# One-hot stationary for 18 fetched node tiles, and the zero fill issued by ScalarE in the two-stack passes

## What is computed

```python
deg = segment_sum(ones, edge_dst, n)
norm = dinv[edge_src] * dinv[edge_dst]          # dinv = deg ** -0.5
root = einsum('nf,kfg->nkg', x, root_w)
for t in range(3):
    h = einsum('nf,kfg->nkg', x, init_w) if t == 0 else einsum('nkf,kfg->nkg', out, w)
    msg = h[edge_src] * norm[:, None, None]
    h = segment_sum(msg, edge_dst, n)           # the sum over edges
    out = relu(h + root + b)
```

## Time and profile before

| what | value |
|---|---|
| median of 3 timed runs | 3352.11 us (3344.53 to 3356.41) |
| the profiled execution | 3317.19 us, of which its span is 3315.3 |
| pass 0, first to last dense product | 1022.50 to 1471.34 us |
| pass 1 | 1471.34 to 1951.58 us |
| passes 2 to 4 | 1951.58 to some 2764 us |
| busy share of the span | PE 95%, DVE 40%, POOL 25%, ACT 23% |

### The profile page before, as it was taken

How to read it: one execution, slowest core, us unless ns; L and a number is a source line. 1 busy time by engine, 2 the same in 40 slices (tenths; PEclk the granted TensorE clock), 3 DMA queues, 4 the chain that set the end, 5 groups by cost and what they waited for, 6 DMA issues and landing times. The chain is left out here.

```text
span 3315.3 us, 51940 instructions
## 1 busy us (share of the span) xinstructions
PE 3133.6 (95%) x18657; PEld 1902.1 (57%) x18658; DVE 1341.3 (40%) x5159; ACT 771.9 (23%) x1620; POOL 834.1 (25%) x808
## 2 busy tenths in 40 slices
PE   7897999999999999998999999999999999929998
PEld 4464666665655666655666655555555556616775
DVE  7846778777762222222222212222221004624443
ACT  3444555555540000000000000000000002513333
POOL 3100000000003666626566610000000000654555
PEclk9896999999999999999999999999999999959999
DMA  7221554654738777766777768888889996436886
GB/s 192 80 66 60 185 212 161 239 216 161 247 162 314 243 242 242 255 218 213 239 231 249 236 221 282 290 291 292 291 291 321 303 302 195 148 129 176 203 199 138
DMA packets 244598, 723.87 MB, mean 218 GB/s; under 512 B 35343, under 2 KB 153347, under 8 KB 242354
## 3 DMA queue, kind: packets, MB, share of 16 engines
q1 hardware_dynamic: 181140, 609.25, 54.9%
q0 software_dynamic: 48256, 99.18, 10.8%
q10 hardware_dynamic: 15006, 12.82, 1.4%
HBM read 542.84 MB, written 189.35 MB: 221 GB/s over the span
## 5 line engine op out<-in xcount | busy, mean ns | idle before, releaser
L1831 PE MATMUL first_sum<-stage,split 128*128 128x448 f16 x4704 | 949.7, 354 | 1.9 <-DMA split<-fresh_d 1.9
L1831 PE MATMUL first_sum<-stage,other 128*128 128x448 f16 x3332 | 687.2, 353 | 0.0
L1831 PEld LDWEIGHTS first_sum<-stage,split 128*128 128x128 f16 x4704 | 450.1, 98 | 374.3 <-issue 5.3
L1781 PE MATMUL first_sum<-stage,other 128*128 128x448 f16 x2744 | 648.9, 354 | 0.2 <-ACT stage L1323 0.2
L1308 POOL DMA_INDIRECT stage<-fresh_d,lane_two x272 | 261.5, 961 | 1088.1 <-DMA fresh_d<-split 933.4
L1831 PEld LDWEIGHTS first_sum<-stage,other 128*128 128x128 f16 x3332 | 315.1, 98 | 244.7 <-issue 1.4
L1323 ACT ACTIVATE stage<-group_ps 128x392 f16<-128x392 f32 x784 | 385.6, 497 | 295.4 <-PE group_ps L1770 292.1
L1467 DVE TENSOR_SCALAR place<-iota_col,rel 128x196 f16<-128x196 f16 x1568 | 349.3, 266 | 0.0
L1781 PEld LDWEIGHTS first_sum<-stage,other 128*128 128x128 f16 x2744 | 253.7, 98 | 139.4 <-issue 2.0
L1308 POOL DMA_INDIRECT stage<-later_d,lane_two x272 | 261.6, 962 | 217.7 <-PE group_ps L1873 122.5
L1464 DVE TENSOR_TENSOR lanes<-iota_two,lane_two 128x256 f16<-128x256 f16 x784 | 225.7, 288 | 80.8 <-PE group_ps L1770 68.9
(11 more groups left out here) (383 smaller groups left out, 3019.6 us busy)
## 6 DMA issues: line engine op xcount, KB each, us to landing
stage<-adj_d SPq DMA_DIRECT2D x434, 784.0 KB, 4.2
adj_d<-stage SPq DMA_DIRECT2D x14, 5488.0 KB, 18.4
row_d<-slow_rows SPq DMA_DIRECT2D x12, 3340.5 KB, 29.9
other<-pack_d SPq DMA_DIRECT2D x38, 898.0 KB, 4.8
slot_rows<-row_d SPq DMA_DIRECT2D x38, 393.0 KB, 5.6
stage<-root_d SPq DMA_DIRECT2D x28, 448.0 KB, 7.0
xnT_d<-other SPq DMA_DIRECT2D x14, 448.0 KB, 4.2
split<-root_d SPq DMA_DIRECT2D x14, 448.0 KB, 3.9
```

What stands on the lines that cost most here:

```text
L1781: m = mm(acc[b][k][:, 0:WIN], other[:, h, half, k * P:(k + 1) * P], stage[b][:, h, :], start=(h == 0 and half == 0), stop=(h == TILES - 1 ...
L1831: m = mm(acc[b][k][:, 0:WIN], side(t)[:, h, part, k * P:(k + 1) * P], ring[:, i, r, :], start=(h == 0 and part == 0), stop=(h == TILES - 1 ...
```

## The change

The fetched nodes are cut in tiles of 128 instead of strips of 112, and there are 18 of them, 2304 nodes for 1792. Each has 19 chunks: 342 gathers a pass for 272. Windows 5 to 13 are dense, nine for ten; window 5 only in its last 384 columns, as the first 64 belong to the fetched tile 17. In a chunk the one-hot is now the stationary operand and the gathered rows, high and low parts side by side, are the 512 moving columns: one product for four. The sums then have nodes on partitions. ACT (`sums_high`) and DVE (`sums_low`) read them from the bank, scaled, PE turns them with two fp32 products, and DVE adds the roots. One bank holds the sums of all node tiles in turn, so between two node tiles three tiles without a chunk stand in `Course`.

The zero fill is no longer issued by SP in the build but by ACT, six parts in each two-stack pass, at tile 22 of the windows 1 to 6 of the pass. Roots of fetched nodes come per node tile. SP issues the stores of rows at other places, ahead of the ring piece of their step. The setting up of the list takes 3 gathers for 4 on POOL and 10 small transfers for 17 on SP.

```diff
-UNITS = 4
-STRIP = 112
-STRIPS = WIN // STRIP
-STRIP_GROUPS = STRIP // G
-CHUNK = 17
-LISTED = UNITS * STRIPS * CHUNK
+SPARSE = 18
+FIRST_DENSE = SPARSE * P // WIN
+OVERLAP = SPARSE * P - FIRST_DENSE * WIN
+CHUNK = 19
+ABREAST = P // SPARSE
+GATHERS = -(-CHUNK // ABREAST)
+LISTED = SPARSE * CHUNK
...
-    BEGIN, TAIL, LEAD, SETTLE, AFTER, APART = 28, 22, 10, 6, 8, 2
+    BEGIN, TAIL, LEAD, GAP = 30, 30, 10, 3
+    TURN, ADD, PROJECT, AFTER, APART = 3, 5, 9, 8, 2
 
     def __init__(self, windows):
         self.tiles = windows * TILES
-        self.chunk_at = [self.BEGIN + c * (self.tiles - self.BEGIN - self.TAIL) // LISTED for c in range(LISTED)]
-        self.strip_end = [self.chunk_at[(s + 1) * CHUNK - 1] + 2 for s in range(UNITS * STRIPS)]
-        self.row_at = {}
-        for pair in range(UNITS // 2):
-            for u in range(SUB):
-                self.row_at[(pair, u)] = self.strip_end[pair * 2 * STRIPS + -(-(u + 1) * P // STRIP) - 1] + self.SETTLE
+        span = self.tiles - self.BEGIN - self.TAIL
+        self.chunk_at = []
+        for s in range(SPARSE):
+            first, after = (self.BEGIN + n * span // SPARSE for n in (s, s + 1))
+            self.chunk_at += [first + c * (after - first - self.GAP) // (CHUNK - 1) for c in range(CHUNK)]
+        self.summed_at = [self.chunk_at[(s + 1) * CHUNK - 1] for s in range(SPARSE)]
+        self.row_at = {s: at + self.PROJECT for s, at in enumerate(self.summed_at)}
         for n in range(windows):
-            for place, u in enumerate(TAKEN[n % 2]):
-                self.row_at[((n + UNITS) // 2, u)] = (n + 1) * TILES + self.AFTER + self.APART * place
-        self.row_order = sorted(self.row_at, key=lambda row: (self.row_at[row], row))
+            w = n + FIRST_DENSE
+            for place, j in enumerate(fresh_tiles(w)):
+                self.row_at[j] = (n + 1) * TILES + self.AFTER + self.APART * place
...
     def piece_after(self, x):
-        return x // PT + PIECES + 1
+        return x // PT + PIECES - 1
...
-                    if w < CHUNKS:
-                        sp.wait_ge(c_z, 1)
-                        flat = row_d.rearrange("r c -> (r c)").rearrange("(p n f x) -> p n f x", p=P, f=FOLD, x=BLANK)
-                        sp.dma_start(flat[:, w, :, :], blank.unsqueeze(1).broadcast_to([P, FOLD, BLANK])).then_inc(c_blank, 16)
...
+                def sparse_roots(t, s):
+                    S = t * SPARSE + s
+                    if S >= 2:
+                        sp.wait_ge(s_v, S - 1)
+                    sp.dma_start(rin_s[:, s % 2, :, :], root1_d.rearrange("p (k n) -> p k n", k=2)[:, :, s * P:(s + 1) * P]).then_inc(s_in[s % 2], 16)
...
+                def stored_at(n):
+                    at = courses[0].piece_after(courses[0].row_at[SOME[n][-1]] + 2)
+                    return max(at, (ND - 1) * PIECES) if n < PARTED else at
...
                         M = t * ND * PIECES + m
+                        for some in range(len(SOME)):
+                            if M == stored_at(some):
+                                some_out(some)
                         if M >= PIECES:
                             sp.wait_ge(p_free, M - (PIECES - 1))
                             sp.dma_start(ring[:, i, :, :].rearrange("p t n -> p (t n)"), adj_d[DENSE[n], :, i * PT * WIN:(i + 1) * PT * WIN]).then_inc(p_in[i], 16)
...
                     for c in range(LISTED):
                         g = t * LISTED + c
                         if g >= RING:
                             pool.wait_ge(s_used, g - (RING - 1))
                             pool.wait_ge(s_row[g % RING], 16 * (g // RING))
+                        at = listed_at(*divmod(c, CHUNK))
                         nc.gpsimd.indirect_dma_start(got[:, g % RING, :, :].rearrange("p s c -> p (s c)"), None, tables_d[t].rearrange("p j s c -> (p j) (s c)"),
-                                                     bass.IndirectOffsetOnAxis(ap=tab_row[:, c:c + 1], axis=0)).then_inc(s_row[g % RING], 16)
+                                                     bass.IndirectOffsetOnAxis(ap=tab_row[:, at:at + 1], axis=0)).then_inc(s_row[g % RING], 16)
                 for r in range(RING):
...
+                def sums_high(t, s):
+                    S = t * SPARSE + s
+                    if S >= 2:
+                        act.wait_ge(s_pt, S - 1)
+                    act.wait_ge(s_used, t * LISTED + (s + 1) * CHUNK)
+                    nc.scalar.activation(rows_s[:, S % 2, :], group_ps[0][:, 0:D], ACT.Copy, scale=dinv[:, s:s + 1]).then_inc(s_hi, 1)
+
+                def cleared(w):
+                    flat = row_d.rearrange("r c -> (r c)").rearrange("(p n f x) -> p n f x", p=P, f=FOLD, x=BLANK)
+                    act.dma_start(flat[:, w, :, :], blank.unsqueeze(1).broadcast_to([P, FOLD, BLANK])).then_inc(c_blank, 16)
...
                     course = courses[t]
                     for x in range(course.tiles):
+                        if x % TILES == 22 and 1 <= x // TILES <= CHUNKS // 2:
+                            cleared(t * (CHUNKS // 2) + x // TILES - 1)
                         if t == 1:
-                            for n, pair, u in courses[0].rows(x + course.tiles):
-                                row_high(0, n, pair, u)
-                        for n, pair, u in course.rows(x):
-                            row_high(t, n, pair, u)
+                            for n, j in courses[0].rows(x + course.tiles):
+                                row_high(0, n, j)
+                        for s in course.summed(x):
+                            sums_high(t, s)
+                        for n, j in course.rows(x):
...
+                def sums_low(t, s):
+                    S = t * SPARSE + s
+                    one = rows_s[:, S % 2, :]
+                    dve.wait_ge(s_hi, S + 1)
+                    nc.vector.scalar_tensor_tensor(one, group_ps[0][:, D:2 * D], dinv[:, s:s + 1], one, ALU.mult, ALU.add).then_inc(s_ev, 1)
+
+                def sums_hidden(t, s):
+                    S = t * SPARSE + s
+                    one = hid_s[:, S % HELD, :, :]
+                    dve.wait_ge(s_in[S % 2], 16 * (S // 2 + 1))
+                    dve.wait_ge(s_pt, S + 1)
+                    nc.vector.tensor_tensor(one, group_ps[1][:, 0:D].rearrange("p (k n) -> p k n", k=2), rin_s[:, S % 2, :, :], ALU.add).then_inc(s_v, 1)
...
+                    mm(group_ps[0][:, :], hot[:, g % HOTS, :], got[:, g % RING, :, :].rearrange("p s c -> p (s c)"), start=(first == 0),
+                       stop=(first == CHUNK - 1), skip_group_check=True).then_inc(s_used, 1)
+
+                def sums_turned(t, s):
+                    S = t * SPARSE + s
+                    pe.wait_ge(s_ev, S + 1)
+                    if S >= 1:
+                        pe.wait_ge(s_v, S)
                     for k in range(2):
-                        for part in range(2):
-                            m = mm(group_ps[S % 2][:, k * D:k * D + STRIP], got[:, g % RING, part, k * P:(k + 1) * P], hot[:, g % HOTS, :],
-                                   start=(first == 0 and k == 0 and part == 0), stop=(first == CHUNK - 1 and part == 1), skip_group_check=True)
-                    m.then_inc(s_used, 1)
+                        m = nc.tensor.transpose(group_ps[1][:, k * P:(k + 1) * P], rows_s[:, S % 2, k * P:(k + 1) * P], ident[:, :])
+                    m.then_inc(s_pt, 1)
 
...
-                        m = tile_sums(t, n % 2, h, i, r)
+                        m = tile_sums(t, W % 2, h, i, r, OVERLAP if n == 0 else 0)
...
                         for c in course.chunks(x):
                             chunk(t, c)
+                        for s in course.summed(x - Course.TURN):
+                            sums_turned(t, s)
```

388 lines of the change are left out of this document (193 added, 195 removed).

## The result

The changed kernel took 3523.2 us (median of 4, 3521.2 to 3532.1), the kernel before beside it 3348.7 (4 runs, 3344.5 to 3356.4): a ratio of 1.052, interval 1.0495 to 1.0552. Forecast were 3376 us and a range that ended at 3410. The sign was right; 147 us were missing. The profiled run took 3532.1 us, span 3530.3.

The account below looks back on a forecast made before the run. GpSimd's gathers, 342 x 1.262 = 431.6 us a pass, were taken to become the bound. Pass 0 +23.6, pass 1 0, fills and the rest 0 made +24 on the median 3352.1: 3376 us, range 3358 to 3410.

Parts of the forecast that it names:

- 333 pitches later: 420.2: Pass 0: the last gather starts 333 pitches of 1.262 us, 420.2 us, after the ninth, at 1465.9.
- 0 and +20 us: Zero fills moved into the two-stack passes: worth between 0 and +20 us through longer gather landings; taken as 0.
- PE's sum and the bound: Two-stack passes: PE's sum falls 19 us a pass, but GpSimd's 342 gathers, 431.6 us, become the bound.
- the fills choke the gathers: Rival, two-stack passes: landings over 10.1 us make GpSimd stand still, 26 us a pass, 3428 us; chance 0.09.
- The issue costs what a transfer cost SyncE, 0.43 us: ScalarE's fill issues in the passes: 0.43 us each, before rows that come one in several us, so 0.
- nobody holds it: GpSimd's gathers in the catching-up stretch: starts 1.26 us apart with nobody holding it, so a pitch of 1.262 us.
- The 120.9: Pass 0 of the kernel before: GpSimd stands 120.9 us waiting for PE, the cover to watch.
- Between two node tiles PE has three tiles (2.3 us) in which ScalarE and VectorE must read the sum bank: no wait.: Node tile boundaries: ScalarE (0.47 us) and VectorE, much the same, read the bank within 2.3 us; PE waits 0.
- The session of the measurement some 8 either way.: Range of the whole kernel's time: the measurement session shifts it some 8 us either way.
- VectorE holds GpSimd off: Rival, gathers: a 256 ns one-hot before each makes the pitch 1.5, +80 us a pass, 3530 us; chance 0.01.
- What would show it.: Signs: gathers back to back, 0.30 between, releaser "issue"; PE waiting some 40 us for gathers in pass 0; pass 0 about 472 us.

Follow-up runs that it names:

- run 6: The kernel before, unedited, profiled beside the other runs on the same chip: 3317.1 us.
- run 8: The changed kernel with the zero fill issued by SyncE in the build again, timed beside the unedited changed kernel: 3339.3 us, ratio 1.007 to the kernel before.
- run 1: The changed kernel with the zero fill issued by SyncE in the build again, nothing else different: 3337.7 us, kernel before 3312.3.
- run 14: The changed kernel with the fill in the build, two sum banks, later turning and 12 buffers for fetched rows: 3330.2 us, ratio 1.0037 to the kernel before.
- run 13: The changed kernel with the fill in the build, a hand-made late bank release, two sum banks and turning 5 tiles later: 3540.8 us, ratio 1.051.
- run 5: The changed kernel, unedited, timed again beside the kernel before: 3384.2 us, ratio 1.020.
- run 2: The kernel before with only the zero fill moved to ScalarE, 12 pieces in the two-stack passes: 3322.1 us.

## Why the prediction was wrong

The changed kernel came 174 us above the kernel before, 24 were forecast. Of the rest 43 are what it loses in the quick groups too (3384.2 less 3317.1 is 67), the fills above all; 107 go with a condition that the forecast had not. Two steps failed that the time shows: that nobody holds GpSimd, so that its last gather comes "333 pitches later: 420.2", which took 491.2 us; and the fills at "0 and +20 us", which cost 45.

- *PE's sum and the bound.* Right. With the fill in the build and the increments on time the kernel takes 3339.3 for 3317.1, +22, where the sum said +24. Part of that closeness is luck: against the trace of before in the same group (run 6) the two passes are 30 us longer, for 24, and the rest of the kernel is 5 shorter. Pass 0 is 471.3 (forecast 472.4), pass 1 486.5 (480.3). In the first trace the product of 512 columns has its next neighbour 0.22 us after its start (1265.81 to 1266.03), as scaled. GpSimd, in runs 8 and 1:

```profile
L1325 POOL DMA_INDIRECT stage<-fresh_d,lane_two x342: 942/946/1160, 1020.8 to 1458.4; - x171
...
  issue: 134.0, 440
  PE group_ps L1913: 78.9, 206
...
L1325 POOL DMA_INDIRECT stage<-later_d,lane_two x342: 940/946/1362, 1507.1 to 1940.0; - x171
```

  In pass 1 of run 1 341 pitches in 432.9 us are 1.269, for 1.262. In pass 0 of run 8 the last gather starts 441.6 us into the pass, for 443.4. In pass 1 the first comes 17.7 us in, for 20.6, and the last 452.9, for 450.9; the pass is 6 us longer all the same, as the product of the last gather follows 8.1 us behind it (1941.0 to 1949.07) and not 3.9: PE is still at the chunks before it, and does not wait.
- *The bound tested by its size.* Fewer gathers, 304, gave 25 us against run 8, which only made up for what the change costs; spread by the time that PE has for them they gave 17 more, passes of 447.1 and 468.7 in place of 471.3 and 486.5.
- *The fills, "between 0 and +20 us; I take 0".* They cost 45 (3384.2 less 3339.3), well over the range's 20. The rival "the fills choke the gathers" had the mechanism, at 0.09 and 52 us; twelve buffers gave 33 back. With twelve buffers the fills still cost 21 (3351.1 less the 3330.2 of run 14, which has two banks and later turning besides), so some 24 of the 45 hung on the ring's depth. The evidence against it was its weak point: the fill's load is less than the ring's on average, but it comes beside the ring and not in its place, and gathers went from 4.0 to 7.7 us. "The issue costs what a transfer cost SyncE, 0.43 us" was a second error: the fill's own issue takes 0.4, and it is the next ones on its queue that take up to 6.4. The Trainium skill (DMA: Bandwidth & Descriptors, SWDGE vs HWDGE vs iDMA) says that a DMA engine goes round its queues in turn; that the fills would then cost 0 was drawn from it and is not on the page, and the measured 45 decide against it.
- *"nobody holds it", and so a pitch of 1.262 from the ninth gather to the last.* This is the step that failed in the first measurement, 71 of the 73 us in pass 0 and 80 of the 82 in pass 1. It needs PE's increment to be seen at once, each time that a gather waits for a buffer. The cover for it had gone: before, 271 pitches are 342 us of the 415 between the first gather and the last (1026.8 to 1442.0), so GpSimd had 73 us of slack in pass 0. The 120.9 that the prediction reads as its waiting for PE hold 160 waits, and in each the 0.30 that stand between any two gathers. In the changed kernel no slack is left, and the late releases, 131 us in both passes, go into the passes.
- *"Between two node tiles PE has three tiles (2.3 us) in which ScalarE and VectorE must read the sum bank: no wait."* This failed too, with 50.8 us of PE's waits, 6.20 at the place shown. It needs PE's increment to be seen at once and ScalarE to be free. With both, run 8 shows 0.2 us at 36 boundaries. But PE's time was not what set the passes, and without these waits, though with more of its increments late, run 13's passes are as long.
- *What the late increments cost outside the passes.* Against run 5 the span is 147 us longer: 106 in the passes, 34 behind the one-stack passes and 7 before pass 0. The 34 all lie in the first part of the final stage (the windows of the first measurement and of run 5):

```profile
2949.50:3190.00 240.50, 142.60 (x681) 104.54 (x679) 107.12 (x421) 76.36 (x158) 98.51 (x106) 0.79 0.41 135
```

```profile
2836.40:3043.00 206.60, 132.39 (x681) 98.41 (x679) 107.06 (x421) 76.09 (x158) 98.80 (x106) 0.83 0.48 158
```

  There GpSimd writes rows by indirect DMA, and ScalarE reads PE's sums (L2338, L2364) over 0.5 us late in 9 of 28 places, up to 4.7 us; in run 5 in none. The kernel before has this stage too, and its measurements differ by 32 us (3349 to 3317); that these are the same loss is not shown, as it was never traced in that condition. The 7 us are within what the other traces differ by (pass 0 starts at 1016 to 1024 us).
- *The clock of PE* is no term of the prediction. In the first measurement PE is busy 945.7 us in the two passes for 914.4 in run 5 and 897.2 in run 8, with the same products, at a granted clock of 0.95, 0.97 and 0.99. After the waits of 6.20 and 5.48 us shown above it stood at the lower of its two levels (0.61 us for a product of 0.38). Where GpSimd sets the pass, this falls into time that PE would have waited, so it has no price of its own here.
- *"The session of the measurement some 8 either way."* The kernel before alone spread from 3312 to 3371. That the profiled run stood 35 us under the median was a sign: I put the difference on the median, as if it added to both kernels alike.
- *VectorE holds GpSimd off*: no. Gathers beside more one-hots take 946 ns in the median (952 before).
- *What would show it.* The gathers "back to back with 0.30 between" are true of run 8: of all its gaps between gathers 2 in pass 0 and 8 in pass 1 are longer than 0.32 us, the longest in front of the first chunk. The releaser is not always "issue": the 78.9 us in 206 waits for PE in the rows above are, but for some 17, these same 0.30. PE's wait for gathers is 29.9 us in pass 0 (some 40 forecast).

## What to carry to other kernels

A stage is as robust as its tightest round trip: when an edit takes the slack from the second engine, and its buffers are released by another's increments, price it with increments that come some us late, not only with those of one good trace. And read slack from the first and the last start, not from the sum of waits, which holds the gaps that stand there anyway. A bulk transfer is not free because the mean rate fits; ask what landing time the ring can bear while it runs, and what else its queue's engine must do behind it. And when the run of before in one session differs by 1% from that in another, measure the unedited change again before explaining it: here four edits each seemed to cure what had gone by itself.

## What the runs showed of the hardware

- PE's semaphore increments were seen up to 7.7 us late in three of the traces, in the two-stack passes and in the first part of the final stage (there up to 4.7 us in the first measurement, 7.4 in run 13), both with GpSimd's indirect DMAs beside them; the instructions' own durations were as ever (gathers 949 ns, the one-stack passes 813.3 us for 813.3). The one-stack passes show nothing of it; the kernel before's own 450 us passes were never traced in that condition. In the same three traces over a third of the semaphore records is missing (22,992, 23,786 and 22,398 for 36,728 in run 5). Whether the records and the lateness have one cause, and whether the lateness would be there without the recording, is not known; every timed execution was recorded.
- The condition came and went on one chip: the kernel before 3371 us in one group, 3315 in a later one.
- Behind a 3.3 MB fill on the same engine's queue, a DMA issue of 0.6 to 0.7 us took up to 7.0 us in the changed kernel and up to 17.3 in run 2, and ScalarE was held meanwhile.
- Beside such a fill a gather of 128 rows of 1 KB lands in 7.7 us instead of 4.0, and a piece of 784 KB in 10.4 instead of 4.2.
- A window of 192 columns ran at its columns: 0.33 us for its four products, 0.757 for four of 448.
